# One kernel, two blocks or one: a graph network whose first block is merged into the main one

## What is computed

```python
def reference(x, src, dst, edge_attr_64, ...):
    # first layer: h = x W (4 heads of 64); e = a_src.h[src] + a_dst.h[dst], leaky;
    # alpha = softmax of e over the edges of one dst; out = sum(alpha * h[src]) W_out
    x = _layernorm(x + _L0_gnn_ref(x, edge_index, W, attn, W_out))
    # second layer: m = x W_n2m^T; q, k, v from m; e from edge_attr; softmax over edges of one dst;
    # out = sum(alpha * (v[src] + e)); x_r = m Wskip^T; beta = sigmoid([out, x_r, out - x_r] Wbeta^T)
    # (beta * x_r + (1 - beta) * out) W_m2n^T
    x = _layernorm(x + _L1_gnn_ref(x, edge_attr_64, edge_index, ...))
    return x
```

## Time and profile before

| | us |
|---|---|
| median of 3 runs | 1283.99 (1282.26 to 1284.12) |
| the profiled execution | 1281.43 |
| its span, first to last instruction | 1279.6 |
| PE busy in the span | 1173.7 (92%) |
| DVE, POOL, ACT busy | 1044.6, 859.4, 828.8 |
| mean granted TensorE clock | 0.977 of full |

### The profile page before, as it was taken

How to read it: one execution, slowest core, us unless ns; L and a number is a source line. 1 busy time by engine, 2 the same in 40 slices (tenths; PEclk the granted TensorE clock), 3 DMA queues, 4 the chain that set the end, 5 groups by cost and what they waited for, 6 DMA issues and landing times.

```text
span 1279.6 us, 28379 instructions
## 1 busy us (share of the span) xinstructions
PE 1173.7 (92%) x6982; PEld 1022.5 (80%) x6982; DVE 1044.6 (82%) x3794; ACT 828.8 (65%) x2783; POOL 859.4 (67%) x1074
## 2 busy tenths in 40 slices
PE   4699999999998699999999799999999995799995
PEld 3688998999897478878888589999999994678884
DVE  3477777777778889999999799999999986789885
ACT  0366666666566866666666756656666668589996
POOL 4688888888883355555554567777777754288888
PEclk9899999999999899999999999999999998799998
DMA  6658888888884388878887677767767743356662
GB/s 173 210 185 276 272 262 265 268 269 264 271 257 150 96 271 260 253 253 251 258 250 243 201 239 217 221 205 220 233 202 219 226 146 110 120 180 189 186 192 94
DMA packets 208795, 276.99 MB, mean 216 GB/s; under 512 B 40044, under 2 KB 140419, under 8 KB 208633
## 3 DMA queue, kind: packets, MB, share of 16 engines
q1 hardware_dynamic: 188793, 224.13, 55.6%
q0 software_dynamic: 19264, 50.85, 13.1%
q10 hardware_dynamic: 576, 0.20, 0.1%
HBM read 159.67 MB, written 117.12 MB: 216 GB/s over the span
## 4 chain that ended last, share of the span: by engine, by line
PE 59%; DVE 15%; issue 12%; POOL 7%; ACT 3%; DMA 1%; another core or an unknown queue 1%; DVEq 0%; SPq 0%; POOLq 0%; ACTq 0%
PE banks L744 20%; PE banks L857 7%; PE banks L734 6%; PE banks L1385 5%; POOL out L1538 4%; PE banks L847 3%; PE banks L1220 3%; POOL output_r L1544 3%; DVE AT L1246 3%; PE banks L859 3%; PE banks L1372 2%; PE banks L1390 2%; PE banks L1213 2%; PE banks L946 2%; PE banks L1370 2%
## 5 line engine op out<-in xcount | busy, mean ns | idle before, releaser
L744 PE MATMUL banks<-m_ext,node_XT 128*128 128x257 f32 x1568 | 376.6, 383 | 0.0
L744 PEld LDWEIGHTS banks<-m_ext,node_XT 128*128 128x128 f32 x1568 | 284.9, 192 | 33.1
L770 DVE SCALAR_TENSOR_TENSOR node_X<-banks,node_be,node_X 128x256 f32<-128x256 f32 x392 | 169.8, 475 | 81.7 <-ACT node_be L696 53.0
L671 POOL TENSOR_TENSOR node_r<-node_vv,half 128x4 f32<-128x4 f32 (+1 forms) x202 | 213.8, 1058 | 17.2 <-POOL node_vv L666 0.3
L702 ACT ACTIVATE node_XT<-banks 128x512 f32<-128x512 f32 x196 | 117.3, 599 | 131.2 <-PE banks L734 123.5
L666 POOL TENSOR_SCALAR node_vv<-node_mv 128x4 f32<-128x4 f32 (+1 forms) x202 | 59.4, 294 | 191.9 <-DVE node_mv L778 172.6
L709 ACT ACTIVATE node_sq<-node_X 128x256 f32<-128x256 f32 x392 | 157.8, 408 | 0.0
L683 ACT ACTIVATE node_X<-node_X,node_r 128x256 f32<-128x256 f32 x326 | 146.0, 497 | 1.4 <-POOL node_r L671 1.4
L763 DVE BATCH_NORM_STATS2 node_st<-node_X 128x6 f32<-128x256 f32 x392 | 145.6, 414 | 1.3 <-issue 0.5
L734 PE MATMUL banks<-ident,node_X 128*128 128x128 f32 x784 | 122.4, 279 | 19.3 <-issue 10.8
L824 POOL DMA_INDIRECT ring<-in_x,src_col x100 | 107.0, 1070 | 34.1 <-issue 14.1
(11 more groups left out here) (265 smaller groups left out, 2743.7 us busy)
## 6 DMA issues: line engine op xcount, KB each, us to landing
node_X<-in_x SPq DMA_DIRECT2D x196, 256.0 KB
out<-node_X SPq DMA_DIRECT2D x196, 256.0 KB
ring<-rows SPq DMA_DIRECT2D x210, 128.0 KB
rows<-ring SPq DMA_DIRECT2D x100, 256.0 KB
rows<-ring SPq DMA_DIRECT2D x200, 128.0 KB
MB<-keeps SPq DMA_DIRECT2D x40, 320.0 KB, 4.7
store<-rows SPq DMA_DIRECT2D x90, 128.0 KB
MB<-picks SPq DMA_DIRECT2D x50, 128.0 KB
```

Of the source, the lines that this page charges most:

```text
L671: pool.tensor_tensor(r[:, s % 4, NT * lo:NT * hi], v, self.c.half[:, NT * lo:NT * hi], ALU.pow).then_inc(self.roots, 1)
L744: last = pe.matmul(ps[:, NT * o + k, 0:D + 1], self.XT[:, o, k * D + h * P:k * D + (h + 1) * P], c.m_ext[:, h, :], start=(h == 0), stop=(h ...
L770: last = dve.scalar_tensor_tensor(out=X[:, n % U, k, :], in0=ps[:, b + k, 0:D], scalar=self.be[:, n % 4, k:k + 1], in1=X[:, n % U, k, :], ...
```

## The change

The first block is gone. Its instructions are now methods of a class `Head`, and each engine emits them at the head of its share of the main block, ahead of the plan. What the block's end had ordered is ordered by waits on four semaphores: `idx_in`, `heads_in` (the heads' weights and `attn`), `weights_in` (the other 19 loads) and `edges_in`, and by `columns`, which counts ACT's three column copies. ACT now issues W_edge ahead of the biases and, behind its column copies, Wbeta and W_out; SP issues the rest. DVE waits for three columns before stage 0, POOL for two before its first gather, PE for three and for all weights before stage 1. `MADE_AT` moves stage 2 from tile 0 to tile 1, behind tile 0's transposes. And SP's load of node step n below 15 (step s = n - 4) now waits until `measured` has come to s - 1, that is until DVE has measured the row six steps earlier.

```diff
-def head_pass(nc, c, ctx, io):
...
-    with nc.Block() as block:
-        @block.sync
...
+class Head:
+    HEADS, WEIGHTS, EDGES, POOL_DONE = 16 * 3, 16 * 19, 16 * 4, 11
...
+    def sync(self, sp):
...
+            for k in range(2):
+                sp.dma_start(w.w_m2n[:, k, :], io["L1_gnn_W_m2n"][k * P:(k + 1) * P, :]).then_inc(self.weights_in, 16)
+            sp.dma_start(w.w_e, io["L1_gnn_We"]).then_inc(self.weights_in, 16)
+            sp.dma_start(w.w_n2m, io["L1_gnn_W_n2m"]).then_inc(self.weights_in, 16)
+            sp.wait_ge(self.dve_done, 4)
...
+    def scalar(self, act):
...
+            for k in range(2):
+                act.dma_start(w.w_edge[:, k, :], io["L1_gnn_W_edge"]).then_inc(self.weights_in, 16)
...
+            act.wait_ge(self.turned, 1)
             for k, out in enumerate((c.src_col, c.dst_col)):
...
+                act.activation(out[:, :], c.psum[:, 0, k * 256:k * 256 + TILES], ACT.Copy).then_inc(self.columns, 1)
+            act.activation(c.src_next[:, :], c.psum[:, 0, 0:TILES], ACT.Copy, bias=1.0).then_inc(self.columns, 1)
+            for k in range(3):
+                act.dma_start(w.beta[:, k:k + 1], io["L1_gnn_Wbeta"][:, k * DM:(k + 1) * DM].rearrange("a d -> d a")).then_inc(self.weights_in, 16)
             for k in range(2):
...
+                act.dma_start(c.wo[:, k, :], io["L0_gnn_W_out"][k * P:(k + 1) * P, :]).then_inc(self.weights_in, 16)
+
+    def pool(self, pool):
...
+        own.done()
+        assert own.n == self.POOL_DONE
+        pool.wait_ge(self.columns, 2)
...
+        dve.wait_ge(self.dve_done, 8)
+        dve.wait_ge(self.columns, 3)
...
             if s == 1:
-                pe.wait_ge(c.ldd, LOADS)
+                pe.wait_ge(self.head.weights_in, Head.WEIGHTS)
+                pe.wait_ge(self.head.columns, 3)
...
             if s == 0:
-                dve.wait_ge(c.ldd, LOADS)
+                dve.wait_ge(self.head.heads_in, Head.HEADS)
+                dve.wait_ge(self.head.pool_done, Head.POOL_DONE)
...
             if s == 1:
+                dve.wait_ge(self.head.weights_in, Head.WEIGHTS)
...
             if live(s, -self.AHEAD, NSTEPS):
                 n = s + self.AHEAD
+                if n < U:
+                    at_least(sp, self.measured, s - 1)
                 at_least(sp, self.moved[n % U], 32 * (n // U))
                 load(n)
...
-MADE_AT = (-5, -5, 0, 2, 4)
+MADE_AT = (-5, -5, 1, 2, 4)
...
-        head_pass(nc, c, ctx, io)
         main_pass(nc, c, io, out)
```

More of the change, by code:

```diff
@@ L155, in __init__ @@
         self.picked = take(TILES, P)
-LOADS = 16 * (1 + 4 + 6 + 3 + 1 + 3 + 4)
-EDGE_LOADS = 16 * 4
-def head_pass(nc, c, ctx, io):
[L164 to L170, removed]
-    with nc.Block() as block:
-        @block.sync
[L174 to L207, removed]
-            for k, out in enumerate((c.src_col, c.dst_col)):
[L209 to L248, removed]
-            for k in range(2):
-                last = pe.transpose(c.psum[:, 0, k * 256:k * 256 + TILES], w.row[:, k, :], c.ident[0:TILES, 0:TILES])
-            last.then_inc(turned, 1)
@@ L258, with __init__ @@
     SPREAD, FUSED, MIXED = 20, 25, 28
-    def __init__(self, nc, c, ctx):
-        self.c = c
+    def __init__(self, nc, c, ctx, head):
+        self.c, self.head = c, head
         def sem(name):
@@ L441, in emit @@
             if s == 0:
-                dve.wait_ge(c.edge_loads, EDGE_LOADS)
+                dve.wait_ge(self.head.edges_in, Head.EDGES)
                 for out, into in ((w.prevf, w.previ), (w.nextf, w.nexti), (w.posf, w.posi)):
@@ L1679, in main_pass @@
         c.load_keeps = load_keeps
-        made = Weights(nc, c, ctx)
-        masks = Masks(nc, c, ctx)
+        head = Head(nc, c, ctx, io)
+        made = Weights(nc, c, ctx, head)
+        masks = Masks(nc, c, ctx, head)
         positions = Positions(nc, c, ctx, masks)
@@ L1701, in _ @@
             def _(sp):
+                head.sync(sp)
                 emits = [p.sync(sp) for p in parts]
@@ L1707, in _ @@
             def _(pool):
+                head.pool(pool)
                 emits = [p.pool(pool) for p in parts]
@@ L1713, in _ @@
             def _(pe):
+                head.tensor(pe)
                 emits = [p.tensor(pe) for p in parts]
@@ L1719, in _ @@
             def _(act):
+                head.scalar(act)
                 emits = [p.scalar(act) for p in parts]
@@ L1725, in _ @@
             def _(dve):
+                head.vector(dve)
                 emits = [p.vector(dve) for p in parts]
@@ L1790, in build @@
         c = Core()
-        c.ldd = c.semaphore(nc, ctx, "ldd")
-        c.edge_loads = c.semaphore(nc, ctx, "edge_loads")
         def sb(name, shape, dt=F32):
```

62 lines of the change are left out of this document (added).

## The result

The changed kernel takes **1277.04 us** (median of 7 runs, 1276.12 to 1299.82; the longest was a disturbed one) beside 1284.12 of the kernel before (7 runs): a ratio of **0.9947, 95% interval 0.9924 to 0.9971**. The forecast was 1266.0 within 1261 to 1278. The direction is right and the time lies in the range, but the gain is 7 us instead of 18, and the time is that of the rival "The stop comes back" (1277.8), which had a chance of 0.25.

The account below looks back on a forecast made before the run. TensorE was taken to bound the kernel from 58 us on, so the start decides: marker 58.1 to 40.1 saves 18.0 us, from 1281.4 to 1263.4, plus 2.6 to stand beside the median: 1266.0 us, range 1261 to 1278.

Parts of the forecast that it names:

- The stop comes back: Rival: PE's signal of the first score product is again held 10.2 us; gain 6.2 us, 1277.8 us; chance 0.25.
- The stop goes: Early main block: the joint standstill of PE, ACT and DVE, 29.63 to 39.82 us before, would vanish and PE run on.
- full DMA does it is my inference: Assumed cause of PE's signals reaching ACT and DVE ten us late: DMA full from 28 to 31 us, share 1.06.
- marker: Second node step's transposes on PE, at 58.14 us before; waits for everything the change moves; predicted at 40.1 us.
- All weights in at 11.0, bounds 10.1 and 13.7: Start: all weight loads landed by 11.0 us, 13.7 before; the bounds change the forecast by -0.9 or +2.7 us.
- The serial chain behind the weights: PE and DVE weight stages, first tiles and products, running on from weights in at 11.0 to the marker at 40.1 us.
- DVE's products hidden: DVE's heads' weight products, 8.05 to 11.5 us, hidden behind the weights' arrival plus PE's transposes.
- Gathers from 5.9 to 7.2, 22.5 us for 18: POOL's first gather at 5.9 us or up to 1.3 later instead of 14.48; its 18 requests take 22.5 us.
- Gather requests held up by DVE: Rival: POOL's requests slowed beside DVE's weight work, 2.2 us a request; whole gain lost, 1284 us; chance 0.03.
- Steps of the node rows at nothing: SP's node-row loads waiting for DVE's measuring of the row six steps earlier, costed at nothing.
- Late node rows: Rival: nine SP row loads make DVE wait and TensorE starves; at 3 us each 1293 us; chance 0.05.
- Gain carried by TensorE-bound work: From 58 to 390 us TensorE is busy 330.66 of 332 us, so an earlier start ends the kernel equally earlier.

Follow-up runs that it names:

- e1: Changed kernel with SP's first node-row loads held until DVE is through weight stage 2: 1276.36 us, ratio 0.9948 to the kernel before.
- e2: Changed kernel with POOL's string of 18 gather requests broken (tile n < 10 waits until PE has transposed tile n - 5): 1269.64 us, ratio 0.9881.
- e6: e2 with W_edge, Wbeta and W_out issued by SP again, so one queue: 1271.53 us, ratio 0.9897.
- e10: e6 without the step-by-step node-row requests, leaving the merged block, the moved stage and the broken string: 1269.82 us, ratio 0.9867.
- e8: e2 without the step-by-step node-row requests: 1270.7 us, ratio 0.9884.
- e3: Changed kernel without the step-by-step requests; SP asks for the first fifteen node rows as before the change: 1277.98 us, ratio 0.9955.
- e5: Kernel before the change with only the edit of e2, POOL's gather requests broken: 1277.91 us, ratio 0.9955.
- e7: e2 with POOL's first gather held until the heads' weights and attn are in: 1274.49 us, ratio 0.9915.
- e9: e2 with weight stage 2 back at tile 0, ahead of tile 0's transposes: 1276.19 us, ratio 0.9926.
- e4: Changed kernel with POOL's first gather held until all weights are in: 1283.09 us, ratio 0.9988 to the kernel before.
- e11: Changed kernel with the edit of e2 using n - 6, so POOL pauses after 16 requests: 1282.5 us, one run.
- e12: Changed kernel with the edit of e2 using n - 5, so POOL pauses after 14 requests: 1269.15 us, one run.

## Why the prediction was wrong, step by step

- **The stop goes: wrong, and it is most of the miss.** The sum priced the stop's end at "if the stop goes, PE runs on", 10.2 us of its 18. What made me think that it goes was the step "full DMA does it is my inference", taken from one stretch of three us. e1 shows the stop without full DMA and e2 full DMA without the stop. What decides is POOL's string of gather requests, which the change only moved earlier, and PE's work moved with it into the string's second half. Its price in the changed kernel: marker 53.38 - 44.39 = 9.0 us, median 1277.04 - 1269.64 = 7.4. The row that would have told it stood in front of me: the last early request ends at 37.02 and the engines go on 2.8 us later; I used that row for the gathers' speed only. With the next two terms this accounts for the marker: 40.1 + 5.4 (weights) - 1.1 (chain behind them) + 9.0 (stop) = 53.4.
- **All weights in at 11.0, bounds 10.1 and 13.7: wrong, 16.38.** I carried over issue times and landing times from a kernel with one busy queue ("1.38 + 1.06 = 2.44 us", "lands 2.3 us after"). Beside a second queue and the gathers, W_out took 3.24 us to issue instead of 1.06, and W_n2m's data came 6.58 us after its issue by the chain. The upper bound was "as today", though nothing excluded a loss. e6 and e10 show the term at 14.28 and 14.04 on one queue: beside the early gathers the change's second queue costs 1.4 us (e8 against e10) to 2.1 (e2 against e6) where I had it win 2.7 (13.7 to 11.0). The Trainium skill (DMA: Bandwidth & Descriptors, "Issuing engines are not separate DMA queues") says that issuing from several engines only saves issue time on the sequencer; here not even that held, as the issue of We rose from 0.43 us (e6) to 1.08 (e8) and more, 2.33 in the changed kernel.
- **The serial chain behind the weights: right.** Predicted 40.1 - 11.0 = 29.1 us from the weights to the marker if nothing stops; e2 measured 44.39 - 16.37 = 28.0, e10 28.9 with 1.4 of a held signal in it. Its parts too: 4.5 us for stage 2 predicted and measured (20.85 to 25.35), and 2.7 from the end of PE's weight transposes to stage 2, with tile 0's transposes in the gap, against 2.85 predicted. Tile 1 and the first product took less (25.28 to 27.17, 1.9 us instead of 3.3), by luck: the transposes ran in 0.66 us instead of 1.09, a rate that only the bounds allowed for. The bound laid it to the clock, but the granted clock from 25 to 28 us is 1.00 in both kernels, so the cause is not shown.
- **DVE's products hidden: right, by luck.** attn landed 7.2 us after its issue instead of 5.5, and DVE began at 10.23 instead of 8.05; the weights were later still.
- **Gathers from 5.9 to 7.2, 22.5 us for 18: right** (6.69, and 22.6 us). The rival "Gather requests held up by DVE" did not come: a request took 0.94 to 1.16 us all through, beside DVE's copies too, so the lock of the Trainium skill (SBUF — State Buffer, "SBUF: two separate sides") is not seen in this stage. It is hardly put to the test either: the page names fp32 copies within SBUF, and DVE's long copies here read PSUM banks. The 1.16 us that I laid to DVE is that of a first request: it took as long here at 6.69, with DVE idle until 10.23. What I called "not on the path" was wrong in another way: the requests were not late, they made others late.
- **Steps of the node rows at nothing: right** (e3, e8). "Late node rows" did not come.
- **Gain carried by TensorE-bound work: right** (330.46 of 332 us).
- **The rival "The stop comes back": right in its time** (marker 51.9 predicted, 53.38 measured; 1277.8 and 1277.04) by two errors that nearly cancel: the weights came 5.4 us later than it assumed, and the hold, now of stage 2's signal instead of the product's, was 6.8 us (25.35 to 32.17), not 10.2. The time lies closer still than the marker because the forecasts stand beside the median of before, 2.6 us above its profiled execution, and the changed kernel's median does not lie above its own: luck again.

So the account of the change is: with the string unbroken it wins 7 us. With the same line added to both kernels the difference is 8 us (e5 1277.91, e2 1269.64), 6.3 at the marker (50.66, 44.39), but the two signals still held in e5 cost that kernel up to 4.9 us, and e2 has none; by these numbers I estimate 1 to 3 us for the merged block and the moved stage (e2 44.39 or e10 42.92 against 50.66 - 4.9 = 45.8). The rest would be the held signals. No run shows the kernel before free of held signals. The second queue and the steps win nothing that can be seen; the stop, which one line removes, stays.

## What to carry to other kernels

A wait that ends on nobody is a cause still to be found: before a sum rests on its going, look at what every other engine was doing when it ended, in each place where it occurs, and price its staying as the first case. An engine off the critical path can hold up others by doing its work too early and in one go; here one wait that breaks its string of requests won 6 us in the kernel before, about as much as the whole restructuring. Where the breaks fall counts, and no safe number of requests was found: strings of twelve held a signal in e7 and e10, one of six in e9. And issue and landing times of DMAs hold for the load at which they were read: a second queue that shares the same engines can make both longer. And when the same edit is tried in two kernels, look for what it leaves in each before their difference is put down to something else.

## What the runs showed of the hardware

- While POOL issues indirect gathers in one unbroken string, signals of PE to ACT, DVE and POOL come late from some point on. Early in the string they passed, up to 12.9 us in (before: ACT at 27.41, string from 14.48); in other runs signals 10.8 us in (e4) and 11.0 us in (e5) were held already. In a second string a signal 5 us in was held (e9). The hold ended 2.2 to 2.9 us after the last request in before, after, e1, e3, e4, e7, e10, e11 and e12, and 1.2 to 1.6 after it behind the shorter strings of e5 and e9; a few signals came earlier (e1 and e4 inside the string). ACT's signal to PE passed in the meantime, by the timing in e4. That the string does it is shown by e2, e5, e11 and e12, where nothing else was changed; whether it is the requests themselves or the transfers that they start, why the first us of a string hold nothing, and, as the ends of matmuls are modelled, whether PE's signal or the end of its work comes late, was not told apart and stays open.
- With seven of SP's loads moved to ACT's queue, issues took longer: We 1.08 to 2.33 us, against 0.43 (e6, e10) and 0.50 (before) with all seven on SP's; the last two loads of SP 3.21 to 5.01 us, against 0.97 (before) to 1.50 (e10). It is not only that both issue at once: in the changed kernel ACT's last issue ended at 9.05 and SP's 4.84 us began at 10.74. The cause is not shown.
- Behind the stop, with TensorE idle from 27.17 to 34.10, the granted clock was at its lower level of 1.2 GHz (0.51 from 32 to 39 us); without the stop it was 1.00 through the same stretch (e2).
